# Stacking the late queries of two heads for the last 64 keys in the first attention's two short tiles, with the engines' lists laid anew

## The reference

```python
q = jnp.einsum('bsd,dhe->bshe', resid, W_Q)
k = jnp.einsum('bsd,dge->bsge', resid, W_K)
v = jnp.einsum('bsd,dge->bsge', resid, W_V)
scores = jnp.einsum('bqgre,bkge->bgrqk', q, k) / jnp.sqrt(jnp.float32(D_HEAD))
causal_mask = jnp.triu(jnp.ones((seq, seq), bool), k=1)
scores = jnp.where(causal_mask, jnp.float32(-1000000.0), scores)
probs = jax.nn.softmax(scores, axis=-1)
z = jnp.einsum('bgrqk,bkge->bqgre', probs, v)
```

## Time and profile before

| | |
|---|---|
| time, median of 3 runs | 1151.18 us (1151.14 to 1151.82) |
| the profiled execution's own time | 1151.44 us |
| its span, first to last instruction | 1149.6 us |
| PE busy | 1132.4 us, 98% |
| DVE busy | 1040.9 us, 91% |
| ACT busy | 1001.2 us, 87% |
| POOL busy | 958.5 us, 83% |
| mean granted clock of TensorE | 0.998 of full |

### The profile page before, as it was taken

How to read it: one execution, slowest core, us unless ns; L and a number is a source line. 1 busy time by engine, 2 the same in 40 slices (tenths; PEclk the granted TensorE clock), 3 DMA queues, 4 the chain that set the end, 5 groups by cost and what they waited for, 6 DMA issues and landing times.

```text
span 1149.6 us, 45236 instructions
## 1 busy us (share of the span) xinstructions
PE 1132.4 (98%) x17504; PEld 820.2 (71%) x17504; DVE 1040.9 (91%) x4019; ACT 1001.2 (87%) x3168; POOL 958.5 (83%) x950
## 2 busy tenths in 40 slices
PE   9999999999999999999999999999999999999987
PEld 7677666777678676777676776777767777666765
DVE  7898899999999899999989899998998989999984
ACT  6888889888899889889898998989888898997795
POOL 2787888889888898888978889888978898988855
PEclk9999999999999999999999999999999999999999
DMA  6001010000110100111001101001001010011010
GB/s 233 11 12 33 16 32 22 21 16 9 31 27 5 45 14 3 41 25 39 14 3 36 38 23 32 17 4 42 9 23 26 4 28 23 14 35 29 11 33 27
DMA packets 31094, 31.85 MB, mean 28 GB/s; under 512 B 12576, under 2 KB 21408, under 8 KB 30752
## 3 DMA queue, kind: packets, MB, share of 16 engines
q1 hardware_dynamic: 30448, 28.17, 9.3%
q10 hardware_dynamic: 432, 0.79, 0.2%
HBM read 10.07 MB, written 2.10 MB: 11 GB/s over the span
## 4 chain that ended last, share of the span: by engine, by line
PE 83%; DVE 6%; POOL 5%; issue 2%; ACT 2%; DMA 0%; SPq 0%; POOLq 0%; DVEq 0%; ACTq 0%
PE psum L496 39%; PE psum L535 11%; PE psum L571 11%; PE psum L548 7%; PE psum L649 5%; PE psum L680 4%; PE psum L631 2%; PE psum L664 2%; DVE prob L898 1%; POOL x_hat L1164 1%; POOL rnorm L1135 1%; PE psum L594 1%; DVE b_prob L980 1%; ACT b_prob L803 1%; POOL b_prob L1152 1%
## 5 line engine op out<-in xcount | busy, mean ns | idle before, releaser
L747 ACT ACTIVATE prob<-prob,negmax 128x512 f32<-128x512 f32 (+3 forms) x512 | 282.7, 558 | 16.1 <-DVE negmax L898 15.3
L898 DVE CUSTOM_DVE_ANT_0 prob<-psum,causal 128x512 f32<-128x512 f32 (+3 forms) x512 | 224.0, 484 | 11.5 <-PE psum L535 9.6
L1102 POOL TENSOR_SCALAR prob<-prob,rowinv 128x384 f32<-128x384 f32 (+1 forms) x256 | 161.2, 649 | 50.1 <-DVE rowinv L904 48.7
L803 ACT ACTIVATE b_prob<-b_prob,b_negmax 128x128 f32<-128x128 f32 x512 | 199.0, 395 | 0.8 <-DVE b_negmax L980 0.7
L496 PE MATMUL psum<-wqkv,h_t 128*64 128x512 f32 x768 | 190.8, 599 | 0.1
L535 PE MATMUL psum<-k_t,q_t 64*128 64x384 f32 (+3 forms) x1024 | 163.5, 443 | 0.7 <-DVE prob_t L910 0.6
L1122 POOL TENSOR_TENSOR r<-r 128x512 f32<-128x512 f32 x120 | 153.4, 1284 | 7.0 <-DVE r L938 6.9
L571 PE MATMUL psum<-prob_t,v 128*64 128x256 f32 x1280 | 153.1, 380 | 0.0
L980 DVE CUSTOM_DVE_ANT_0 b_prob<-psum,band,rnorm 128x128 f32<-128x128 f32 x512 | 145.8, 344 | 5.4 <-PE psum L649 4.9
L1152 POOL TENSOR_TENSOR b_prob<-b_prob,b_rowinv 128x1024 f32<-128x1024 f32 x61 | 116.0, 1902 | 27.7 <-DVE b_rowinv L1000 27.6
L1105 POOL TENSOR_TENSOR prob<-prob,rowinv 128x512 f32<-128x512 f32 x96 | 98.1, 1047 | 36.4 <-DVE rowinv L904 36.3
(11 more groups left out here) (104 smaller groups left out, 2725.6 us busy)
## 6 DMA issues: line engine op xcount, KB each, us to landing
vb_mid<-vb SPq DMA_DIRECT2D x112, 128.0 KB, 2.4
x_t<-in_x_t SPq DMA_DIRECT2D x8, 256.0 KB, 3.9
x_n<-in_x SPq DMA_DIRECT2D x8, 256.0 KB, 3.1
x<-x SPq DMA_DIRECT2D x64, 31.8 KB
out<-x SPq DMA_DIRECT2D x15, 128.0 KB, 1.8
wqkv<-in_wqkv SPq DMA_DIRECT2D x1, 1536.0 KB, 11.3
w<-in_w SPq DMA_DIRECT2D x1, 768.0 KB, 13.1
x<-x SPq DMA_DIRECT2D x48, 0.2 KB
```

Of the source, the lines that this page charges most:

```text
L747: last = af(pr, pr, ACT.Exp, bias=negmax[:, k % 4, o:o + 1], scale=-1.0, accum_out=rowsum[:, k % 4, o:o + 1])
L803: last = af(pr, pr, ACT.Exp, bias=b_negmax[:, a, o:o + 1], scale=-1.0, accum_out=b_rowsum[:, a, o:o + 1])
L898: vec.tensor_tensor_reduce(prob[:, k % PROBS, h, p * K:(p + 1) * K], bank[:, p * K:(p + 1) * K], causal[:, S - K:S], -E ** -0.5, 3.0e38, A ...
L1102: last = gp.tensor_scalar(pr, pr, rowinv[:, k % 4, h:h + 1], 1.0, ALU.mult, ALU.mult)
```

## The change

In tiles with `i` in `JOINT = (0, 1)`, two neighbouring pairs with the same keys, called even and odd, are scored together. The tokens of the even pairs are projected with the two halves of the tile exchanged, late first, so that their queries stand turned in `q_t`. A further copy, `q_late`, holds 64 late queries of the even pair and 64 late queries of the odd one side by side. The last 64 keys are streamed once against `q_late` for both; the even pair is streamed against the first `K - 64` keys, and the odd pair against the same keys in blocks of 64, each with a matmul of its own, so that the shared block can stand next to both. The masks, the views in `maxima` and the transposed probabilities in `value` follow the exchange, and `value` does one pair a time there. The lists of all engines, the banks and the numbers of idle matmuls are different.

```diff
+JOINT = (0, 1)
-WARM = (3, 2, 2, 4, 2, 4, 3, 2, 1, 9, 2, )
+WARM = (6, 3, 4, 2, 4, 3, 3, 6, 2, )
...
+        def even_at(i, p):
+
+            return p // 2 * 3 * E + E if i == 0 else 0
+
+        def odd_at(i, p, block):
+
+            return p // 2 * 3 * E if i == 0 else (6 - block) * E
...
+                tokens = x_t[:, b % 2, i * P:(i + 1) * P]
+                turned_tokens = tokens.rearrange("p (q n) -> p q n", q=2)[:, ::-1, :]
                 for c in range(4):
-                    last = halves(bank[:, c * P:(c + 1) * P], wq[:, 4 * h + c, :], x_t[:, b % 2, i * P:(i + 1) * P])
+                    moving = turned_tokens if i in JOINT and c % 2 == 0 else tokens
+                    last = halves(bank[:, c * P:(c + 1) * P], wq[:, 4 * h + c, :], moving)
...
-                for p in range(np_):
+                queries = q_t[:, (NT * b + i) % 2, :, :]
+                for p in range(0, np_, 2 if i in JOINT else 1):
+                    keys = k_t[:, b % 2, (c + p) // 2, 0:K]
                     for h in range(2):
-                        last = mm(banks[h][:, p * K:(p + 1) * K], q_t[half(h), (NT * b + i) % 2, c + p, :],
-                                  k_t[half(h), b % 2, (c + p) // 2, 0:K], start=True, stop=True)
+                        if i not in JOINT:
+                            last = mm(banks[h][:, p * K:(p + 1) * K], queries[half(h), c + p, :], keys[half(h)], start=True, stop=True)
+                            continue
+                        even, odd = queries[half(h), c + p, :], queries[half(h), c + p + 1, :]
+                        both = q_late[half(h), i, (c + p) // 2, :]
+                        place = even_at(i, p)
+                        mm(banks[h][:, place:place + K - E], even, keys[half(h), 0:K - E], start=True, stop=True)
+                        mm(banks[h][:, place + K - E:place + K], both, keys[half(h), K - E:K], start=True, stop=True)
+                        for x in range(2 * i + 1):
+                            at = odd_at(i, p, x)
+                            last = mm(banks[h][:, at:at + E], odd, keys[half(h), x * E:(x + 1) * E], start=True, stop=True)
...
-                for p in range(0, max(np_, 2), 2):
+                for p in range(0, max(np_, 2), 1 if i in JOINT else 2):
...
-                copy(q_t[:, (NT * b + i) % 2, 4 * h:4 * h + 4, :].rearrange("p c n -> p (c n)"), bank).then_inc(q_act, 1)
+                last = copy(q_t[:, (NT * b + i) % 2, 4 * h:4 * h + 4, :].rearrange("p c n -> p (c n)"), bank)
+                if i in JOINT:
+                    last = copy(q_late[:, i, 2 * h:2 * h + 2, :].rearrange("p d (x n) -> p d x n", n=E), late_of(bank))
+                last.then_inc(q_act, 1)
```

## The result

| | before | after |
|---|---|---|
| time, median | 1151.50 us (4 runs, 1151.14 to 1151.96) | 1194.86 us (4 runs, 1194.20 to 1195.47) |
| the profiled execution's own time | 1151.44 us | 1195.30 us |
| its span | 1149.6 us | 1193.4 us |

The ratio is 1.0376, with a 95% interval of 1.0358 to 1.0394: the change costs 43.4 us. The forecast was 17.5 us (1169 against 1151.5). The sign was right, and the time lies in the stated range, but the size is two and a half times the forecast one.

A forecast was written before the change was run, and what follows sets the result against it. PE, busy 98% of the span, was taken to bound the kernel. Scores +7.0 and +10.8, values +0.8, lists and idle matmuls -0.9 gave +17.7 us on 1151.44, so 1169 us, range 1160 to 1222.

The forecast's parts named there:

- PE bounds, and the extra work is all on it: Whole kernel: PE is busy 98% of the span, so each microsecond it gains or loses is one of the span.
- The load of 128 float32 columns sets the step at 0.11 us: Scores: with streams of 64 columns, the weight load and not the streaming (0.055 to 0.066 us) sets each step.
- The halves side by side over a whole unit: Score units: both array halves work at once, 12 steps in tile 0 and 10 in tile 1; chance 0.54.
- a reach that is enough for six but not for ten: Rival on scores: TensorE looks past six waiting records to the other half but not ten; 1175 to 1210 us, 0.14.
- the rival of 1220 us: Scores: the halves run one behind the other, only last and first matmul overlapping; +68.6 us, chance 0.15.
- Tile 0: Scores of tile 0: 12 steps of 0.110 us for 8, 0.44 us more in each of 16 units, +7.0 us.
- Tile 1's bare loads: Scores of tile 1: 2 steps of 0.160 us and 8 of 0.110, 0.34 us more in 32 units, +10.8 us.
- Values: Products with values, tiles 0 and 1: each step of 256 columns becomes two of 128, at most +0.8 us.
- Copies: Further query copies, 16 each on ACT and DVE: costed at nothing, being covered; 6.4 us in all without cover.
- Lists: Engine lists: seven fewer changes of shape, -0.7 us, and one idle call fewer, -0.2 us.
- bounds of -4 and +3 us: Limits set on what the new lists could win or lose by shorter or longer waits; zero in the sum.
- the fourth of four parts passes the second records of three others: Sign in the local attention's 64*64 scores: four matmuls start together, taken as evidence against the halves running one behind the other.

The follow-up runs named there:

- Splitting alone: Kernel before, each tile 0 score matmul of 128 streamed columns done as two of 64 with the same weights: 1164.69 us, ratio 1.0117.
- four and then six: Changed kernel, tile 1 units ordered as four records of each half (even and shared), then six of each (odd blocks): 1176.27 us, ratio 1.0223.
- alternating halves: Changed kernel with only its score matmuls reordered, so that the two halves take turns with every matmul: 1167.58 us, ratio 1.0142.
- new lists alone: Kernel before with only the lists, banks and idle matmuls of the changed kernel: 1153.19 us, ratio 1.0011.
- values and copies alone: Kernel before with values of tiles 0 and 1 one pair a time and the further query copies to an unread buffer: 1153.14 us, ratio 1.0014.
- tile 1 alone: Kernel with one odd matmul and alternating halves, but only tile 1 scored jointly and tile 0 as before the change: 1153.44 us, ratio 1.0020.
- one odd matmul: Kernel with alternating halves, the odd pair's three blocks of tile 1 merged into one matmul of 192 columns: 1159.99 us, ratio 1.0071.
- four in a row: Kernel before, tile 1 units doing both pairs of half 0 first, then both of half 1: 1152.51 us, ratio 1.0012.

## Why the prediction was right or wrong

*PE bounds, and the extra work is all on it:* right. PE's busy time and the span grew alike, both by 43.8 us.

*The load of 128 float32 columns sets the step at 0.11 us:* right. Splitting alone cost 13.6 us for a forecast 14, and the step is 0.112. The load of 188 ns, the same as before, says it in the trace.

*The halves side by side over a whole unit:* this is the step that failed. The prediction costed 12 and 10 steps for both halves together. In a tile 1 unit the second half started 0.78 us late. The arrangements with runs in a row agree on where the second half begins: with the seventh record of ten, the fifth of eight, the third of six and the first of four. With four and then six, its first odd record comes with the seventh of the first half's ten. In each, three records of the first half still wait ahead of it. With alternating halves the same work took 27.3 us less.

The time of 1194.86 us lies where the prediction put "a reach that is enough for six but not for ten" (0.14, 1175 to 1210 us). That rival comes near to what happened but is not it: a reach of three is too short for six records as well, only less so. Neither half was wholly behind the other, as the rival of 1220 us has it.

The smaller terms can be checked apart from waits and clock. PE's busy time is from the pages. What of it fell in stretches at half clock is from windows, and half of that is taken off, which is an estimate. The last column is the span less the busy time.

| kernel | PE busy | of it at half clock | at full clock | not busy |
|---|---|---|---|---|
| before | 1132.4 us | 0 | 1132.4 us | 17.2 us |
| new lists alone | 1133.5 | 3.2 | 1131.9 | 18.0 |
| values and copies alone | 1133.2 | 0 | 1133.2 | 18.1 |
| tile 1 alone | 1134.3 | 5.8 | 1131.4 | 19.0 |
| one odd matmul | 1140.3 | 3.4 | 1138.6 | 19.5 |
| alternating halves | 1147.6 | 0 | 1147.6 | 18.1 |
| the change | 1176.2 | 3.0 | 1174.7 | 17.2 |

*Tile 0:* +6.5 us in the times between the kernels with and without it, 7.2 us in PE's work, for a forecast 7.0, with alternating halves. How much of the 27.3 us is tile 0's was not tried by itself.

*Tile 1's bare loads:* 7.6 us in the times by the merged odd blocks, 9.0 us in PE's work, for a forecast 10.8. One of the ten steps is half as long as costed. In the trace of the alternating kernel the shared block's first record starts at 31.544 and its second at 31.600, since the first one's load, begun at 31.383, had run under the 192 columns before it. So 0.054 us a unit, 1.7 us in 32, were costed too much. Why the times show less of the saving than the work is open.

*Values:* +0.8 us of PE's work, as forecast. *Copies:* no work on PE, and at most the one wait at 103.5 us.

*Lists:* -0.5 us of PE's work for a forecast -0.9, but about +1.8 us in the time. In the profiled executions with the new lists TensorE waits at some 21 us for the input's transfer (`DMA x_t<-in_x_t`, 1.4 us with the new lists alone, 1.2 to 3.2 in the others), which none with the old lists does. And a wait near the end is 1.8 us long for 1.0 before (`PE psum L680 <- issue`); soon behind it, from 1126.5 us, the clock is at half for 3.4 us. The prediction's bounds of -4 and +3 us took in such waits; that a wait can be followed by half the clock is in none of its terms. Each kernel has one trace, so how much of this is in the medians is not shown. Of the 11 executions with the new lists alone the one with a mean granted clock of 1.000 was the fastest, 1150.61 us, and those below 0.998 took 1153.8 and 1154.9.

So the costed kernel, at 1167.6 us for 1169, is no proof of every term: PE's work grew by 15.2 us for 17.7, and 0.9 us of waiting came on top.

The differences of the times, order of halves 27.3, three odd blocks 7.6, tile 0 6.5 and 1.9 for what is left (1153.44 against 1151.49), add up to 43.3 because each starts where the last one ends; that is no check of them. In PE's work at full clock they are 27.1, 9.0, 7.2 and -1.0.

The reading that would have found it was there. The prediction saw that in the earlier trace rows the fourth of four parts passes the second records of three others, and took that as a sign of a long reach. The row shows a reach of three and not of more, and runs of six and ten had to be held against that number instead of against "reaches" or "does not reach". The Trainium skill's rule in "TensorE: Matmul & The Clock Gate", section "The mechanism", that matmuls start strictly in program order, does not hold between parts here: it would have made four in a row cost 21 us, and it cost 1.4.

That nothing is left to gain also follows from the measured prices. In tile 1 one matmul against the shared block takes the place of 128 of 512 streamed columns of two heads, the last 64 keys of each. It streams 64, but its load of 128 columns takes 0.11 us, as long as 128 columns stream. The kernel with tile 1 alone agrees: its PE work at full clock is 1131.4 us, against 1131.9 with the new lists alone.

## What to carry to other kernels

Count a float32 matmul's price as the longer of its stream and its weight load, per part of the array, each read from the trace at hand; narrowing streams below the width of the weights gained nothing here and added loads. Transposes are another case: with weights of 128 columns they went at 0.064 us a step. When parts of the array work side by side, write the program so that they alternate with every matmul, or check the trace for instants at which only one part's matmuls are in flight. And when a row shows that something is passed or hidden, read how much of it, and compare that with how much the change asks for. Before a microsecond or two is called work, look in the trace for waits, and for stretches at half clock behind them.

## What the runs showed of the hardware

TensorE starts a matmul on one half of the array past waiting matmuls of the other half, up to three records of them. The second half began with the first record of four in a row (1.4 us in 32 units), with the fifth of eight (+7.2 us over 16 units), with the third of six, and with the seventh of ten, 0.78 us late. Whether the three are counted in all or for each part is open; the four parts of the 64*64 scores, which start together, fit both.

Float32 weight loads of 128 columns follow each other at 0.11 us on a half, and with 64 streamed columns the steps are 0.112 us; a shorter one, 0.056 us, stood behind a stream of 192 columns, under which a load had run. A transpose with weights as wide goes at 0.064 a step.

The granted clock fell to half for 6.8 us in a wait of TensorE of 3.2 us (tile 1 alone, at 20 us), and for 3.4 us behind waits of 2.2 us (one odd matmul), 1.8 us (new lists alone) and 2.0 us (the change). Waits of 2.2 and 1.7 us in the kernel with alternating halves were not followed by it.
